# Attention scores as fp32 matmuls in four row groups, with queries, keys and values kept in SBUF

## The reference, cut to what matters

```python
h = _ln(x) * (1 + sc_msa) + sh_msa                    # stage 1: projection, attention 1 (8 windows of 128)
scores = einsum('bnqhd,bnkhd->bnhqk', q, k) / 4; attn = softmax(scores); x = x + (attn @ v @ w_so + b_so) * g_msa
...
top_s, top_i = top_k(scores, 16)                      # stage 2: attention 2, 154 keys
attn = softmax(top_s); o = sum of attn * v[top_i]; x = x + (o @ w_co + b_co) * g_mca
x = x + (silu(a) * b @ w_m2 + b_m2) * g_mlp           # stage 3, hidden 1024
h = mha(h, h, ...)                                    # stages 4 and 5: attention 3, 1024 x 1024 a head
h = mha(h, context, ..., mask=mask)                   # stages 5 and 6: attention 4, 154 keys, masked
x = x + gelu(h @ w1 + b1) @ w2 + b2 + t_mlp           # stage 6
```

## Time and profile before

| | |
|---|---|
| median of 3 runs | 1883.4 us (1880.19 to 1887.14) |
| the profiled execution | 1880.98 us |
| its span, first to last instruction | 1878.9 us |
| PE, DVE, ACT, POOL busy | 73%, 54%, 41%, 16% of the span |
| DMA | 103.65 MB |

### The profile page before, as it was taken

One profiled execution on the slowest core, in us unless ns is written; L12 is line 12 of the kernel. 1 busy time (PEld: TensorE's weight loads), 2 busy tenths in 40 slices (PEclk: granted clock), 3 DMA queues, 4 the chain that ended last, 5 costly groups with the idle time before them and its releaser, 6 DMA issues.

```text
span 1878.9 us, 22617 instructions
## 1 busy us (share of the span) xinstructions
PE 1371.0 (73%) x7052; PEld 697.2 (37%) x7052; DVE 1006.3 (54%) x2985; ACT 776.6 (41%) x1626; POOL 307.1 (16%) x518
## 2 busy tenths in 40 slices
PE   2746557464556677756678989999879977778988
PEld 1324345332334334433333424322422214333556
DVE  4444335465776555565476556777777715643120
ACT  0213224244554445434123544566546673444221
POOL 7010010324444322232310000100010000100110
PEclk9958778675556989877699989999999998888999
DMA  4496873203111011012910031252313021440000
GB/s 159 147 162 141 134 126 82 43 26 78 22 22 25 1 22 22 1 40 81 129 18 1 1 55 48 77 100 29 45 43 46 13 42 22 87 65 6 12 15 23
DMA packets 115851, 103.65 MB, mean 55 GB/s; under 512 B 25115, under 2 KB 95504, under 8 KB 115476
## 3 DMA queue, kind: packets, MB, share of 16 engines
q1 hardware_dynamic: 114844, 101.82, 28.6%
q10 hardware_dynamic: 887, 0.39, 0.1%
HBM read 69.95 MB, written 31.63 MB: 54 GB/s over the span
## 4 chain that ended last, share of the span: by engine, by line
PE 38%; DVE 9%; issue 4%; DMA 2%; ACT 2%; SPq 2%; POOL 1%; ACTq 0%; DVEq 0%; POOLq 0%
PE bank L811 6%; PE bank L782 6%; PE bank L746 5%; PE ring L708 5%; PE ring L725 5%; DVE part_max L1200 3%; PE ring L661 2%; PE ring L685 2%; DVE x_hat L1174 1%; ACT pr L1003 1%; PE bank L814 1%; PE bank L816 1%; PE bank L752 1%; DMA ks<-ctx_mask 1%; PE ring L692 1%
## 5 line engine op out<-in xcount | busy, mean ns | idle before, releaser
L1003 ACT ACTIVATE pr<-bank 128x512 f32<-128x512 f32 x656 | 366.2, 596 | 259.7 <-PE bank L782 191.0
L1200 DVE TENSOR_REDUCE part_max<-bank 128x1 f32<-128x512 f32 x512 | 325.0, 684 | 169.5 <-PE bank L746 168.5
L746 PE MATMUL bank<-ks,qs 96*128 96x512 bf16 x512 | 197.4, 393 | 35.9 <-DVE part_max L1200 27.0
L782 PE MATMUL bank<-qs,ks 100*128 100x512 bf16 x512 | 195.0, 387 | 27.7 <-ACT pr L1003 16.0
L842 PE MATMUL bank<-ident,probs 128*128 128x128 f32 x256 | 58.5, 370 | 130.8 <-POOL probs L1339 130.6
L1234 DVE MAX8 top<-bank 128x8 f32<-128x154 f32 x256 | 69.9, 314 | 133.2 <-PE bank L831 133.0
L811 PE MATMUL bank<-pr,vs 128*32 128x512 f32 x1024 | 137.7, 610 | 1.0 <-ACT pr L1003 1.0
L1020 ACT ACTIVATE exp_all<-bank,neg 128x154 f32<-128x154 f32 x256 | 85.1, 387 | 111.3 <-POOL neg L1328 110.5
L708 PE MATMUL ring<-h_t,w_m 128*128 128x512 f32 x256 | 131.0, 639 | 0.0
L782 PEld LDWEIGHTS bank<-qs,ks 100*128 100x128 bf16 x512 | 48.3, 97 | 215.1 <-ACT pr L1003 159.0
L1273 POOL TENSOR_SCALAR var_eps<-mean_var 128x4 f32<-128x4 f32 x24 | 5.8, 241 | 729.3 <-DVE mean_var L1165 728.9
(11 more groups left out here) (153 smaller groups left out, 2275.6 us busy)
## 6 DMA issues: line engine op xcount, KB each, us to landing
qs<-q_dram SPq DMA_DIRECT2D x192, 128.0 KB
q_dram<-parts SPq DMA_DIRECT2D x32, 384.0 KB, 2.5
ks<-k_dram SPq DMA_DIRECT2D x96, 128.0 KB
v_dram<-v_out SPq DMA_DIRECT2D x32, 256.0 KB, 2.9
vs<-v_dram SPq DMA_DIRECT2D x16, 512.0 KB
k_dram<-parts SPq DMA_DIRECT2D x16, 384.0 KB, 2.6
w_m<-in_L_xcond_w_m SPq DMA_DIRECT2D x1, 2048.0 KB, 9.7
w_m<-in_L_xcond_w_m SPq DMA_DIRECT2D x2, 1024.0 KB, 6.4
```

The source lines that it names most:

```text
L746: last = nc.tensor.matmul(bank[:, :], qs[0:PACK, h, t * P:(t + 1) * P], ks[0:PACK, h, kc * 512:(kc + 1) * 512], start=True, stop=True)
L782: last = nc.tensor.matmul(bank[:, :], ks[0:FULL, h, kt * P:(kt + 1) * P], qs[0:FULL, h, qc * 512:(qc + 1) * 512], start=True, stop=True)
L1003: nc.scalar.activation(m.pr[:, u % NPR, :], m.bank[2 + u % 2][:, :], ACT.Exp).then_inc(m.s_free, 1)
L1200: nc.vector.tensor_reduce(m.part_max[:, slot, i // 2, i % 2:i % 2 + 1], bank[:, :], axis=AX.X, op=ALU.max).then_inc(m.m_read, 1)
```

## The change

Queries and keys stay in SBUF as fp32. A projection's 128 channels hold eight heads, two in each 32 rows. Two copies are made from the PSUM bank, one with the odd heads zeroed and one with the even heads zeroed (scale `marks`, bias `padded`), so that every head lies alone in 32 rows; a free row of them carries the maximum, one the mask. Groups are now of every second head, and a head's score is one fp32 matmul over its 32 rows. ACT makes both copies for half of the units (`qk_a`), DVE for the others (`qk_d`). The three bf16 parts, `hi`, `split`, `m_split`, all stores to and loads from DRAM of q, k and v, and POOL's fills are gone; only the keys, values and mask of attention 4 go out once and come back (`stash`, `reload`). Values stand in SBUF in 17 columns a head. The maxima are copied once and go by one DMA into four rows. Attention 4's 26 last keys are one matmul over 128 rows (`kt`).

Steps `m` and `s` take the four heads in turn, shifted by two, so that neighbours use different row groups. Banks are no longer fixed: `finish` gives each step one of a set (five shared by `m` and `s` in attention 3, three for top-k scores), and moves the reading step ahead where it has to. In the lists of a stage the reading step now stands one place after its matmul. `o_turn` and `o_norm` run group by group, behind each half of an attention group. Times in the plan are new, and top-k walks half of the tokens through all groups before the other half.

```diff
-Q_PART = (0, 1, 0, 2, 1, 0)
-K_PART = (0, 0, 1, 0, 1, 2)
-PACK = 16 * len(Q_PART)
+def banks_of(step):
+    kind = step[0]
+    if kind in ("m", "m_turn", "s"):
+        return (2, 3, 4, 5, 6) if attention(step[1]) == 3 else (3, 4, 5, 6)
+    if kind == "c_score":
+        return (2, 3, 4)
...
     if s == 3:
         for j in range(HT):
-            out.append([("ua", s, b, n, j), ("ua_copy", s, b, n, j)])
+            out[j].append(("ua", s, b, n, j))
+            out[j + 1].append(("ua_copy", s, b, n, j))
...
             elif at == 3:
-                h, t, kc = i // 16, i // 2 % 8, i % 2
-                last = nc.tensor.matmul(bank[:, :], qs[0:PACK, h, t * P:(t + 1) * P], ks[0:PACK, h, kc * 512:(kc + 1) * 512], start=True, stop=True)
+                t, kc, h = i // 8, i // 4 % 2, (i + 2) % 4
...
+                k, rows = m.k_of[at, b, gi % GB], slice(HW * h, HW * h + HW)
+                last = nc.tensor.matmul(bank[:, :], q[rows, t * P:(t + 1) * P], k[rows, kc * 512:(kc + 1) * 512], start=True, stop=True)
...
-                last = nc.tensor.matmul(bank[:, :], ks[0:FULL, h, kt * P:(kt + 1) * P], qs[0:FULL, h, qc * 512:(qc + 1) * 512], start=True, stop=True)
+                k, rows = m.k_of[at, b, gi % GB], slice(HW * h, HW * h + HW)
+                last = nc.tensor.matmul(bank[:, :], k[rows, kt * P:(kt + 1) * P], q[rows, qc * 512:(qc + 1) * 512], start=True, stop=True)
...
-                last = nc.tensor.matmul(m.bank[v % 2][:, hh * C:hh * C + S2], m.qs[gi % 3][0:PACK, h, t * P:(t + 1) * P],
-                                        m.ks2[:, gi % 2, h, 0:S2], start=True, stop=True)
+                last = nc.tensor.matmul(bank[:, hh * C:hh * C + S2], m.q2[b][rows, u, t * P:(t + 1) * P], m.kc[rows, u, hh, b, :], start=True, stop=True)
...
-    for i in range(3):
-        nc.gpsimd.memset(m.qs[i][PACK:FULL, :, :], 1.0).then_inc(m.fills, 1)
...
-        elif kind == "load_qk":
...
-            for r in range(len(Q_PART)):
-                sp.dma_start(m.qs[slot][r * D:(r + 1) * D, :, :], m.q_dram[at][Q_PART[r], r0:r0 + HG * D, :].rearrange("(h d) t -> d h t", d=D)
...
-                plan.at(t0 - 1.2 * step, ("c_score", gi, t, hf))
+                        plan.at(t0 - 1.6 * step, ("c_score", gi, t, hf))
-            plan.at(t1 + 0.3 * step, ("c_turn", gi, t))
-            plan.at(t1 + 0.6 * step, ("c_copy", gi, t), ("c_pv", gi, t))
+                    plan.at(t1 + 0.9 * step, ("c_tail", gi, t), ("c_turn", gi, t))
+                    plan.at(t1 + 1.3 * step, ("c_copy", gi, t))
+                    plan.at(t1 + 1.8 * step, ("c_pv", gi, t))
...
-    plan.spread(token_slots(3, 0), A2 + 66.5 * step, A2 + 112 * step)
+    three = [block_slots(3, 0, n) for n in range(2)]
+    plan.spread(three[0][0] + three[0][1], A2 + half + 6 * step, A2 + 2 * half + 6 * step)
+    plan.spread(three[1][0] + three[1][1], A2 + 2 * half + 6.1 * step, A2 + 3.5 * half)
```

More of the change, by code:

```diff
@@ L167, in token_slots, with group_run @@
+def token_slots(s, b):
+    (head0, tail0), (head1, tail1) = block_slots(s, b, 0), block_slots(s, b, 1)
+    out = [[] for _ in range(len(head0) + len(tail0) + len(tail1))]
+    for i, steps in enumerate(head0 + tail0):
+        out[i] += steps
+    for i, steps in enumerate(head1 + tail1):
+        out[len(out) - len(head1) - len(tail1) + i] += steps
     return out
-def group_run(plan, a, start, width, lead, ready):
+def group_run(plan, a, start, width, lead, late):
     ns, nm, npv = S_UNITS[a], M_UNITS[a], PV_STEPS[a]
@@ L483, in __init__, with free @@
-        for step in plan.steps:
-            if step[0] == "s":
-                self.s_of.append(step[1:])
+        self.s_of = [step[1:] for step in plan.steps if step[0] == "s"]
+        self.o_order = [step[1:] for step in plan.steps if step[0] == "o_copy"]
     def bank(self, *step):
-        return self.m.ring[self.plan.order[step] % 3]
+        return self.m.bank[self.plan.bank[step]]
+    def free(self, *step):
+        return self.m.free[self.plan.bank[step]]
     def freed(self, *step):
-        r = self.plan.order[step]
@@ L631, in tensor_program @@
         elif kind == "o_turn":
-            _, s, b, t = step
-            pe.wait_ge(*g.o_copies(s, b, t // 4))
-            since(pe, g.ring_turn(*step))
-            for q in range(GB):
-                last = nc.tensor.transpose(bank[:, q * P:(q + 1) * P], m.o_t[b][:, q, t * P:(t + 1) * P], m.ident[:, :])
+            _, gi, half = step
+            i = plan.n("o_copy", gi, half)
+            pe.wait_ge(m.o_copied, i + 1)
+            for t in range(4):
+                last = nc.tensor.transpose(bank[:, t * P:(t + 1) * P], m.o_st[:, i % 2, t * P:(t + 1) * P], m.ident[:, :])
             last.then_inc(m.p_mm, 1)
@@ L854, in tensor_program @@
             for h in range(HG):
-                last = nc.tensor.matmul(out[h * HW:(h + 1) * HW, :], m.vs[:, vslot, 0, h * HW:(h + 1) * HW], m.probs_t[:, h * P:(h + 1) * P],
+                last = nc.tensor.matmul(out[h * HW:h * HW + VE, :], m.vc[:, b, gi % GB * HG + h, :], m.probs_t[:, h * P:(h + 1) * P],
                                         start=False, stop=True, skip_group_check=True)
             last.then_inc(m.pv_done, 1)
-def plan_turn(gi):
-    return sum(1 for k in range(gi) if attention(k) != 2 and k % 3 == gi % 3)
@@ new lines, in vector_program @@
+            dve.wait_ge(*g.ran("ck", u))
+            if u == 1:
+                dve.wait_ge(m.rows_stored, 16)
+                dve.wait_ge(m.mask_stored, 16)
+                dve.wait_ge(m.bias_done, 2)
+            for odd in range(2):
+                out = (m.kc_late if x else m.kc)[:, mt, odd, :, :].rearrange("p b t -> p (b t)")
+                last = nc.vector.tensor_scalar(out, g.bank("ck", u)[:, 0:B * S2], m.marks[:, odd:odd + 1],
+                                               m.padded[:, PADDED.index("k4" if x else "k2"), odd, mt:mt + 1], ALU.mult, ALU.add)
```

1285 lines of the change are left out of this document (612 added, 673 removed).

## The result

The changed kernel takes 2393.2 us (median of 4 runs, 2378.5 to 2405.1) where the kernel before took 1881.8 beside it (1878.5 to 1887.1): 1.271 times the time, 95% interval 1.263 to 1.279. The forecast was 1467, with a range of 1335 to 1720. It was wrong in sign and in size. The profiled execution of the changed kernel took 2378.5 us, with a span of 2376.8.

A forecast was written before the change was run, and what follows sets the result against it. No engine was full before attention 3, in top-k engines waited for each other; PE was busy 552 of 635 us in attention 3. Savings 159 + 134 + 40 + 78 + 5 = 416 left a span of 1463, time 1467, range 1335 to 1720.

The forecast's parts named there:

- Prices: Matmuls on PE: 512-column fp32 costs 0.86 us; four over 32 rows each cost about as much as one.
- Start: Before attention 1: fills go, first x_hat at 14 us instead of 37.5, attention 1 starts near 50.
- Attention 1: Start and attention 1: 334 us falls to 175, minus 159, bounds minus 184 and minus 94; PE 100 shared, 183 not.
- Top-k: Top-k stage: 564 us falls to 430, minus 134, with PE the bound; bounds minus 184 and minus 44.
- opened ring: Top-k: in-order waits between engines open through later transposes, copies and products and three banks; part of minus 134.
- Attention 3: Attention 3 stage: 635 us falls to 593, minus 40, with a round of 3.9 us set by banks.
- No sharing: Rival: row strips do not run beside each other; attention 3's round 7.9 us, total 2176; chance 0.07.
- Low clock: Rival: 32-row matmuls leave PE at 1.2 GHz; round 6.4 us, attention 3 about 1040, total 1910; chance 0.07.
- Attention 4: Attention 4 stage: 198 us falls to 120, minus 78, bounds minus 88 and plus 7; PE 113 shared, 205 not.
- The last MLP: Last stage, on PE: 148 us falls by 5, bounds minus 10 and 0.
- Drain: Rival, attention 3: `pv` waits until the last score leaves the array, 0.64 us a round, total 1539; chance 0.15.
- Steps of strips: Rival, attention 3: fp32 matmuls of four strips start 0.43 us apart, round 4.9, total 1650; chance 0.18.

The follow-up runs named there:

- e3: Against the changed kernel, attention 3's score matmuls run over all 128 rows instead of 32 (scores mix four heads): 2360.0 us.
- e2: Against the changed kernel, `m` steps of attentions 1 and 3 take head i % 4 instead of (i + 2) % 4: 1929.7 us.
- e8: On e2, top-k's steps get back their times from the kernel before, relative to the maxima: 2008.8 us.
- e4: Against the changed kernel, all score matmuls of attention 3 run on rows 0 to 31, whichever the head: 3317.9 us.
- e7: On e2, score matmuls of attention 3 take turns on four banks instead of five: 1952.5 us.
- e5: On e2, attention 3's inserted 128-row matmuls of stages 3 to 5 are moved right behind a `pv`: 1906.2 us.
- e9: On e6, attention 3's inserted 128-row matmuls of stages 3 to 5 are moved to the middle of a round: 1864.7 us.
- e6: On e2, neighbouring `m` and `s` units of different strips in attentions 1 and 4 are issued turn by turn: 1864.8 us.

## Why the prediction was wrong, step by step

**Prices.** An fp32 matmul of 512 columns costs 0.86 alone (e3's starts lie 0.86 apart). A set of four strips costs 0.97 before another score and 1.07 before `pv`, at full clock. The 1.07 that I had for it, taken from the length of `pv`'s records, was right, and the 1.72 for two full sets too low. That strips share was right.

**Start.** Right. The first x_hat starts at 15.81 (forecast 14), and the first projection at 20.29; the fills' wait of the earlier trace rows is gone. Attention 1's first score comes at 51 (forecast near 50).

```profile
14.73 1.04 POOL L1307 TENSOR_TENSOR rstd<-var_eps,power 128x4 f32<-128x4 f32 x1
15.81 1.38 DVE L1228 TENSOR_SCALAR x_hat<-x_sb,mean_var,rstd 128x256 f32<-128x256 f32 x4 [1.48 <-POOL rstd L1307]
...
20.29 2.04 PE L726 MATMUL bank<-h_t,wa 128*128 128x512 f32 x2 [1.07 <-ACT h_t L984]
```

**Attention 1.** The step that failed is "128 x 0.86 = 110 us one by one, 27 four at a time", of which I took the 27. The four matmuls of a unit lie on one strip and can't share, and the `s` behind an `m` is on the same strip as well. The new order of heads helps there only where one unit ends and the next begins (e2). In the groups of PE's matmuls from 50 to 345 us the scores are 180 us, where I had 27:

```profile
L818 PE MATMUL bank<-slot 32*128 32x128 f32 x512 | 90.5, 334 | 0.0
L777 PE MATMUL bank<-slot 32*128 32x128 f32 x512 | 89.4, 333 | 0.0
```

Even the bound without sharing, 240, was too low, since it had full clock: 0.77 was granted over the first 345 us. The loads of the earlier trace rows went, as forecast, and PE's own work took their place.

**Top-k.** Right, and for the reason given: 417 us against 430, DVE busy 320 (forecast 318), 3.3 us a step. PE's 381 us are under the forecast's 400 to 450, and e8 shows the opened ring to be worth 88 of the 147 us; the other 59 are not split.

**Attention 3.** Three steps failed. The first is the price of a round, "a bank is held 1.07 for the fp32 matmul" and so 3.9 us: it takes it that neighbours lie on different strips. The round was 10.1 us at half clock and 5.7 at full clock: "No sharing" and "Low clock" stood as two rivals, each with the other's term at its best, and the truth was half of the one together with all of the other. What stood against the low clock, that "PE has hardly a gap", is no argument: in e4 PE was busy 99% at 0.54. Both came from one cause that no rival named, the order of the heads, and the heads of `s` and `m` in the code, followed through the plan's order, would have shown it (the listing of the order ahead names tiles, not rows). With the order mended (e2) the round is 4.3, 0.4 over the model; e7 puts that on the fifth bank, which brings less than the model has. The second is "of the 140 half falls in time in which PE now waits for banks: 70": the inserted work costs 168 in e2 and over 150 in e5 and e9, so in the sum nothing is hidden. The third is "first `m`s at DVE's pace 41": the first group took 87 us from its first `part_max` to the first `pv` in e2, since the MLP of stage 3 runs in the same stretch. By these: 112 x 0.4 = 45, 98 and 46 make 189 of the 199 us that lie between 593 and e2's 792, and the last `s`s, 56 instead of 45, the rest. (593 is also 42 less than 635, where the sum has 40.) The sum for the kernel before had agreed with 635 partly by luck: the stage's true end makes it 646 from its first maximum, and from the first maximum to the first exp it took 84 us and for the last `s`s 50, where I had 95 for both.

**Attention 4.** 222 against 120. PE is busy 211 of it; the "113 shared" took all `m` as shared, but its three 154-column matmuls are on one strip as well. Issued turn by turn (e6) the stage takes 205, which is my bound without sharing. The gain was overstated from the start, too: the 198 us of the kernel before held the last 28 of attention 3, which I read as loads, and 52 of the 99 us of the earlier trace rows are DVE's wait while PE still worked on attention 3 (the wait ends at 1562.8). By its own exps the stage had 170 us to lose from, not 198.

**The last MLP.** 150 against 143: it has the length it had.

**The rivals.** *Drain* held in part. In e2 `pv` starts 1.05 us behind the start of the last score (1402.96 to 1404.01), in the kernel before 0.32 (1263.09 to 1263.41): it does wait until that score has gone through, as the rival says. Of its 0.64 a round at most the 0.4 over the model are there, and no run separates them from the banks' turn. Beyond that a change of shape costs 0.1 us (e3). *Steps of strips* did not hold: halves of four strips start together, 0.53 apart, not one by one. The Trainium skill, "TensorE: Matmul & The Clock Gate", The mechanism, has matmuls start and end in strict order. The records at 1003.8 us disagree for the start: an `s` of another strip started 0.95 us ahead of the `m` that stands before it in the program.

## What to carry over

Where work shares an array by rows, sharing is a property of neighbours: write down, for the order that will run, which rows each matmul uses, before a price for a set is used; one number in the choice of heads was worth 410 us here. Price two rivals together when one cause can bring both, as a matmul alone in its strip brought the low clock. And work inserted beside a stage whose engine waits in pieces of a microsecond is to be priced at its full length until a run shows otherwise: single rounds hid part of it here, the sum did not.
